# The last of three forward Fourier transforms goes from split half precision to float32 products with the data as stationary operand

## What is computed

```
def _L3_conv_ref(x, weights):
    x_f = jnp.fft.rfft2(x)
    k_f = jnp.fft.rfft2(weights)
    out_f = jnp.einsum('bchw,ochw->bohw', x_f, k_f)
    return jnp.fft.irfft2(out_f, s=(H, W))
...
x = x + _L3_conv_ref(_gn(x), L3_conv_weights)
```

## Time and profile before

| | |
|---|---|
| median of 3 runs | 950.18 us (949.63 to 953.7) |
| the profiled execution | 949.47 us, span 947.6 us |
| busy over the span | TensorE 82%, VectorE 63%, ScalarE 55%, GpSimd 13% |
| mean granted clock of TensorE | 0.937 of full speed |

### The profile page before, as it was taken

How to read it: one execution, slowest core, us unless ns; L and a number is a source line. 1 busy time by engine, 2 the same in 40 slices (tenths; PEclk the granted TensorE clock), 3 DMA queues, 4 the chain that set the end, 5 groups by cost and what they waited for, 6 DMA issues and landing times. The chain is left out here.

```text
span 947.6 us, 27147 instructions
## 1 busy us (share of the span) xinstructions
PE 780.6 (82%) x10775; PEld 652.6 (69%) x10775; DVE 599.3 (63%) x1112; ACT 518.9 (55%) x868; POOL 122.4 (13%) x120
## 2 busy tenths in 40 slices
PE   7999996875699464888599999966888488889998
PEld 7999995764588332766444444435777488879997
DVE  3455436678476697689687776775666677752222
ACT  0233337754534270755579998005887557755654
POOL 0000000110100162455103223000000100001110
PEclk9999998898799797889799999997999789999999
DMA  8599968750000100000000000004000448831222
GB/s 308 225 317 382 308 195 215 168 116 4 2 0 0 41 1 0 2 0 0 1 1 1 1 1 1 1 1 107 1 0 0 89 91 183 188 72 54 103 106 93
DMA packets 46066, 80.08 MB, mean 85 GB/s; under 512 B 19619, under 2 KB 38057, under 8 KB 41145
## 3 DMA queue, kind: packets, MB, share of 16 engines
q1 hardware_dynamic: 29368, 62.49, 23.5%
q10 hardware_dynamic: 16640, 16.78, 5.2%
HBM read 50.74 MB, written 27.92 MB: 83 GB/s over the span
## 5 line engine op out<-in xcount | busy, mean ns | idle before, releaser
L1478 DVE SCALAR_TENSOR_TENSOR X<-bank,c_power,X 32x512 f32 x128 | 96.7, 755 | 36.5 <-PE bank L1428 32.9
L930 DVE TENSOR_TENSOR X<-X,bank 128x512 f32 x64 | 43.7, 683 | 91.8 <-PE bank L916 91.8
L1621 PE MATMUL bank<-m_xp,m_kf 128*32 128x64 f32 x2048 | 79.2, 241 | 21.4 <-DVE m_xp L1556 10.0
L1621 PEld LDWEIGHTS bank<-m_xp,m_kf 128*32 128x32 f32 x2048 | 78.2, 171 | 22.7 <-issue 22.5
L433 ACT COPY ks_spec<-bank 128x512 f32<-128x512 f32 x64 | 34.3, 591 | 95.3 <-PE bank L360 92.3
L215 DVE BATCH_NORM_STATS2 bn<-X 128x6 f32 x128 | 83.2, 684 | 2.9 <-POOL X L1218 1.6
L415 DVE COPY ks_rows<-bank 128x512 f32<-128x512 f32 x64 | 41.2, 687 | 66.0 <-PE bank L345 66.0
L1384 ACT ACTIVATE c_r<-X,c_nrm 32x1024 f32 (+1 forms) x56 | 75.4, 1346 | 2.4 <-DVE c_nrm L1452 1.1
L345 PE MATMUL bank<-ks_fw,ks_src 64*128 64x64 f32 x1024 | 68.7, 298 | 6.5 <-DMA ks_src<-in_L_conv_weights 6.5
L345 PEld LDWEIGHTS bank<-ks_fw,ks_src 64*128 64x128 f32 x1024 | 68.1, 215 | 6.4 <-issue 6.4
L360 PE MATMUL bank<-ks_fh,ks_rows 64*128 64x128 f32 (+1 forms) x1152 | 71.1, 277 | 0.4 <-ACT ks_spec L433 0.4
(11 more groups left out here) (189 smaller groups left out, 1870.5 us busy)
## 6 DMA issues: line engine op xcount, KB each, us to landing
ks_src<-in_L_conv_weights SPq DMA_DIRECT2D x16, 1024.0 KB, 7.0
kf<-ks_spec ACTq DMA_DIRECT2D x16, 1024.0 KB, 9.2
m_kf<-kf SPq DMA_DIRECT2D x32, 512.0 KB, 8.3
X<-in_x SPq DMA_DIRECT2D x4, 2048.0 KB, 12.9
out_y<-X SPq DMA_DIRECT2D x16, 512.0 KB, 2.7
l_wb<-in_L_conv_weights_r SPq DMA_DIRECT2D x4, 512.0 KB, 10.8
l_wb<-in_L_conv_weights_i SPq DMA_DIRECT2D x4, 512.0 KB, 13.2
xf<-f_xm SPq DMA_DIRECT2D x16, 112.0 KB, 3.4
```

The costliest lines, as they stand in the source:

```text
L930: dve.tensor_tensor(x, x, ps[4 + c % 4][:], ALU.add).then_inc(added, 1)
L1478: dve.scalar_tensor_tensor(x, of.rearrange("p (y x) -> p y x", x=HN), filt.power[at, 2:3], x, ALU.mult, ALU.add).then_inc(added, 1)
L1621: last = pe.matmul(ps[4 * half + m // 8][at:at + C, m % 8 * N:(m % 8 + 1) * N], kf[p][:, j, :, H * half + m], xp[half][:, j, m].rearrange( ...
```

## The change

The last forward transform no longer uses `Forward`. All of it is in float32:

- The row and column matrices are float32 and come as ks_fw (32 KB), l3_fh and l3_fh0 (256 KB each, the matrix repeated for each row quarter) instead of three pairs of halves (64 KB each).
- f3_src is a ring of four chunks instead of a whole group. Chunks go through only two PSUM banks (0 and 1). A single copy takes the turned chunk to f3_tt, in an order in which each channel's 4 images x 32 rows lie together. Even chunks are copied by ScalarE, odd ones by VectorE.
- Row products: for each channel two products, on partitions 0 to 63 and 64 to 127, with the data as stationary operand (64 x 128) and the matrix moving (64 columns). Eight channels at a time, into banks 2 and 3; VectorE copies bank 2, ScalarE bank 3. The result already has the channels where the column products need them, so there is no second transposition.
- Column products: for each set of 4 slots, 4 parts x 4 images, each on a quarter of 32 partitions, data stationary (32 x 128), matrix moving (128 columns), image b into bank 4 + b, four products added up. Slot 0 has 16 more with 32 stationary columns. Four sets fill the four banks; then VectorE copies banks 4 and 5, ScalarE banks 6 and 7 to xm, each bank with the same step of 128 bytes.
- TensorE's order: a group's eight turns; then its four row blocks of 8 channels, between which the column products of the group before lie (sets 0 and 1 after the first block, 2 and 3 after the second, 4 and 5 after the third); the next group's turns; sets 6 and 7 of the group before. The last group's eight sets come at the end.
- The loop over the groups is written out instead of a hardware loop.

```diff
+    for k in ("l3_fh", "l3_fh0"):
+        out[k] = np.tile(out[k].reshape(C, 2, 2, P), (IB, 1, 1, 1))
...
-        fwd = Forward(pr, ctx, "f3", mats, SLOT_AT, True, {2: 0, 4: 1, 6: 2, 8: 3}, {9: 4, 10: 5, 12: 6, 14: 7})
+    RING, GROUPS, SETS = 4, 4, 2
+    ready_by = [0, 1, 0, 1, 0, 1, 0, 0]
+    read_by = [1, 0, 1, 0, 1, 0, 1, 0]
...
+        src = pr.sb(ctx, "f3_src", [P, RING, CH])
+        tt = pr.sb(ctx, "f3_tt", [P, C, IB, N // 2])
+        rows = [pr.sb(ctx, f"f3_rows{p}", [P, 2, 2 * SLOT, C]) for p in range(2)]
...
+                def turn(q, j):
+                    n = NCH * q + j
+                    pe.wait_ge(ready[ready_by[j]], count(ready_by, ready_by[j], q, j))
+                    if n >= 2:
+                        e = read_by[(n - 2) % NCH]
+                        pe.wait_ge(turned_read[e], count(read_by, e, (n - 2) // NCH, (n - 2) % NCH))
+                    for k in range(4):
+                        m = pe.transpose(ps[n % 2][:, k * P:(k + 1) * P], src[:, n % RING, k * P:(k + 1) * P],
+                                         pr.ident[:])
+                    m.then_inc(turned, 1)
+                def transform_rows(q, g):
+                    n = GROUPS * q + g
+                    for e in range(2):
+                        if g == 0:
+                            pe.wait_ge(turned_read[e], read_by.count(e) * (q + 1))
+                        if n:
+                            pe.wait_ge(rows_read[e], n)
+                    for c in range(C // GROUPS):
+                        for half in range(2):
+                            at = slice(half * N, (half + 1) * N)
+                            m = pe.matmul(ps[2 + half][:, c * N:(c + 1) * N],
+                                          tt[at, C // GROUPS * g + c].rearrange("p b h -> p (b h)"), fw[at],
+                                          start=True, stop=True)
+                    m.then_inc(rows_made, 1)
+                def transform_columns(q, f):
+                    n = SETS * q + f // 4
+                    for e in range(2):
+                        if f == 0:
+                            pe.wait_ge(rows_read[e], GROUPS * (q + 1))
+                        if f % 4 == 0 and n:
+                            pe.wait_ge(kept[e], 2 * n)
+                    def products(slots, mat):
+                        for i, (half, part) in enumerate(np.ndindex(2, 2)):
+                            for b in range(IB):
+                                at, pos = slice(b * C, (b + 1) * C), SLOT * part + 4 * f
+                                m = pe.matmul(ps[4 + b][0:slots * C, f % 4 * P:(f % 4 + 1) * P],
+                                              rows[q % 2][at, half, pos:pos + slots].rearrange("p s c -> p (s c)"),
+                                              mat[at, half, part], start=i == 0, stop=i == 3)
+                        return m
+                    m = products(4, fh)
+                    if f == 0:
+                        m = products(1, fh0)
+                    if f % 4 == 3:
+                        m.then_inc(cols_made, 1)
+                pr.keep_warm(pe, 7)
+                for j in range(NCH):
+                    turn(0, j)
+                for q in range(Q):
+                    for g in range(GROUPS):
+                        transform_rows(q, g)
+                        if q and g < 3:
+                            transform_columns(q - 1, 2 * g)
+                            transform_columns(q - 1, 2 * g + 1)
+                    if q + 1 < Q:
+                        for j in range(NCH):
+                            turn(q + 1, j)
+                    if q:
+                        transform_columns(q - 1, 6)
+                        transform_columns(q - 1, 7)
+                for f in range(SLOT // 4):
+                    transform_columns(Q - 1, f)
...
+            def keep(eng, copy, e, q, u):
+                eng.wait_ge(cols_made, SETS * q + u + 1)
+                for b in (2 * e, 2 * e + 1):
+                    copy(xm[:, 4 * u:4 * u + 4, :, :, IB * q + b].rearrange("p f k r -> p f r k"),
+                         ps[4 + b][:].rearrange("p (f r k) -> p f r k", f=4, r=2)).then_inc(kept[e], 1)
+            def copies(eng, copy, e):
+                def turn(q):
+                    for j in range(NCH):
+                        copy_turned(eng, copy, e, q, j)
+                        if j + RING < NCH:
+                            normalise(eng, e, q, j + RING)
+                for j in range(RING):
+                    normalise(eng, e, 0, j)
+                turn(0)
+                for q in range(Q):
+                    for g in range(GROUPS):
+                        copy_rows(eng, copy, e, q, g)
+                        if g == 0 and q + 1 < Q:
+                            for j in range(RING):
+                                normalise(eng, e, q + 1, j)
+                        if g == 1 and q:
+                            keep(eng, copy, e, q - 1, 0)
+                    if q + 1 < Q:
+                        turn(q + 1)
+                    if q:
+                        keep(eng, copy, e, q - 1, 1)
+                for u in range(SETS):
+                    keep(eng, copy, e, Q - 1, u)
...
-                fwd, fwd_loads = matrices(pr, inner, [(n, [P, 2, P]) for n in ("l3_fw16", "l3_fh16", "l3_fh016")], F16)
+                fwd, fwd_loads = matrices(pr, inner, [("ks_fw", [P, N]), ("l3_fh", [P, 2, 2, P]), ("l3_fh0", [P, 2, 2, P])])
```

More of the change, by code:

```diff
@@ L1487, in l3_forward_stage, with count @@
 def l3_forward_stage(pr, mats, xm, kf0, loaded0):
+    nc, ps = pr.nc, pr.psum
+    fw, fh, fh0 = mats
+    RING, GROUPS, SETS = 4, 4, 2
+    turned, rows_made, cols_made = (pr.sem(f"f3_{n}") for n in ("turned", "rows_made", "cols_made"))
+    ready, turned_read, rows_read, kept = ([pr.sem(f"f3_{n}{e}") for e in range(2)] for n in (
+        "ready", "turned_read", "rows_read", "kept"))
+    ready_by = [0, 1, 0, 1, 0, 1, 0, 0]
+    read_by = [1, 0, 1, 0, 1, 0, 1, 0]
+    def count(by, e, q, j):
+        return by.count(e) * q + by[:j + 1].count(e)
     with ExitStack() as ctx:
-        fwd = Forward(pr, ctx, "f3", mats, SLOT_AT, True, {2: 0, 4: 1, 6: 2, 8: 3}, {9: 4, 10: 5, 12: 6, 14: 7})
-        with pr.nc.Block() as block:
+        src = pr.sb(ctx, "f3_src", [P, RING, CH])
+        tt = pr.sb(ctx, "f3_tt", [P, C, IB, N // 2])
+        rows = [pr.sb(ctx, f"f3_rows{p}", [P, 2, 2 * SLOT, C]) for p in range(2)]
+        with nc.Block() as block:
             @block.sync
@@ new lines, in _, with normalise @@
+                for f in range(SLOT // 4):
+                    transform_columns(Q - 1, f)
+            def normalise(eng, e, q, j):
+                if ready_by[j] != e:
+                    return
+                n = NCH * q + j
+                if n >= RING:
+                    eng.wait_ge(turned, n - RING + 1)
+                of, to = pr.X[:, q, j * CH:(j + 1) * CH], src[:, n % RING]
+                if e:
+                    done = eng.activation(to, of, ACT.Identity, scale=pr.rstd[:, q:q + 1], bias=pr.shift[:, q:q + 1])
+                else:
+                    done = eng.tensor_scalar(to, of, pr.rstd[:, q:q + 1], pr.shift[:, q:q + 1], ALU.mult, ALU.add)
+                done.then_inc(ready[e], 1)
@@ new lines, in copy_turned, with copy_rows @@
+            def copy_turned(eng, copy, e, q, j):
+                if read_by[j] != e:
+                    return
+                n = NCH * q + j
+                eng.wait_ge(turned, n + 1)
+                copy(tt[:, :, :, 4 * j:4 * j + 4],
+                     ps[n % 2][:].rearrange("p (h b c) -> p c b h", h=4, b=IB)).then_inc(turned_read[e], 1)
+            def copy_rows(eng, copy, e, q, g):
+                eng.wait_ge(rows_made, GROUPS * q + g + 1)
+                at = slice(C // GROUPS * g, C // GROUPS * (g + 1))
+                copy(rows[q % 2][:, e, :, at],
+                     ps[2 + e][:].rearrange("p (c n) -> p n c", n=2 * SLOT)).then_inc(rows_read[e], 1)
@@ L1501, in _ @@
             @block.vector
             def _(dve):
-                fwd.low_parts(dve)
+                copies(dve, dve.tensor_copy, 0)
             @block.scalar
             def _(act):
-                fwd.high_parts(act, lambda q, s: act.copy(
-                    xm[:, s, :, :, bass.ds(IB * q, IB)].rearrange("p k r b -> p b r k"),
-                    pr.psum[4 + s % 4][:].rearrange("p (b r k) -> p b r k", b=IB, r=2)))
+                copies(act, act.copy, 1)
 def load_kernel_spectra(sp, pr, to, i, pair, loaded):
```

7 lines of the change are left out of this document (2 added, 5 removed).

## The result

The changed kernel takes 969.55 us (median of 4 runs, 966.13 to 974.55) against 949.9 us (4 runs, 949.15 to 953.7): 1.0193 times as long, 95% interval 1.0159 to 1.0227. It is slower, as forecast, but by 19.6 us instead of 5.3, and outside the range of 945 to 966. The profiled execution took 968.98 us, 19.5 more than that of before.

A forecast was written before the change was run, and what follows sets the result against it. The last forward transform was taken as a chain through TensorE, ScalarE and VectorE, no engine full. Stage +3.35, matrices +0.6, early slow clock +0.4 and tail clock fall +1.7 gave +6.05: 955.5 us profiled from 949.47; range 945 to 966.

The forecast's parts named there:

- The row and column prices: Last forward transform: row products at 0.056 us a record, column products on four quarters at 0.028.
- rival B: Column products: quarters not four times as fast; no better than halves +32, 988 us; halfway +9, 965; chance 0.13.
- halfway: Column products at 0.036 us a record, quarters gaining only part of the speed: +9, 965 us.
- rival C: Last forward transform: shape changes between row tiles cost nothing, not 0.17 us each; -4.1, 951.4 us, no change; chance 0.22.
- rival D: More waiting: VectorE's scattered xm copy at 1.28 us (+4.4), or clock falls in turn stretches; 960 to 963; chance 0.13.
- (g): Larger forward matrices, 352 KB more, loaded in the stats stage ahead: +0.6 us, bounds 0 and 1.2.
- four R, with the row copies uncovered between them: Group 0: four row blocks of 1.79 us with three copy waits of 0.97 between them, 10.07 us.
- Item (i): Tail: TensorE idles 2.2 us twice, one clock fall of 3.2 us counted: +1.7 us, bounds 0 and 3.4.
- turn stretch: A group's eight turns through two banks: 5.11 us of TensorE's queue, 5.28 with a change of shape.
- Keep waits: Column sets share the same four banks, so the next set waits 2.23 us for copies to xm.
- (c): Copy prices: VectorE 0.69 us, ScalarE 0.59; scattered xm copy 1.10, two in 1.95; VectorE's bounds 0.69 and 1.28.
- The first stretch: From the stage's first transposition to its first row product: 6.48 us.

The follow-up runs named there:

- the second trace: The changed kernel run and traced once more, with nothing altered: 970.43 us, ratio 1.0190 to the kernel before.
- Runs 1 and 2: Changed kernel with, first, idle transpositions filling group 0's waits, 963.31 us; second, group 0's row products alternating banks 2, 3 and 4, 5, 958.94 us.
- run 7: Changed kernel plus alternating row banks in group 0, last group's first column sets in banks 0 to 3, two-image xm copies, four-bank turns: 947.21 us, ratio 0.9947.

## Why the prediction was wrong

**What held.** The direction, and the shape of the argument: scarce banks turn work that overlapped into waits. The row and column prices: 0.029 us a record against 0.028 (rival B is refuted by the steady rows; its "halfway" price, 0.036, was not halfway between 0.028 and 0.056, which is 0.042, and nothing hung on it). Changes of shape cost what was forecast, against rival C: in the steady group 702.91 - 700.91 = 2.00 us less 64 x 0.0286 leave 0.17 behind column products, and a row block, 1.93 from its start to the next products (685.13 to 687.06), less 32 x 0.056 leaves 0.14. The 3.07 times that the Trainium skill's table gives for four row tiles (TensorE: Matmul & The Clock Gate, Measured speedup vs the span model) did not show here: against the 0.113 of a product on 128 rows, 0.0286 is 4.0 times as fast, at 128 columns where the table has 512. Turns with gaps (before the third, the fifth and the eighth, where every second one was forecast), waits of 2.2 us twice in the tail, the clock low once behind them at 1.6 us (5.48 against 3.85): nearly as written. In the second trace the clock fell behind both waits, so "once" was in part luck. One of the two waits is put down to VectorE's xm copy, which was rival D's sign: it takes 1.16 us, just over the 1.10 up to which it was to hide. The matrices cost 0.8, within (g)'s bounds.

**The step that failed** is group 0's: "four R, with the row copies uncovered between them (4 x 1.79 + 3 x 0.97 = 10.07)". The waits were priced right and taken for plain idle time. Item (i) let the clock fall only behind idle times of 2 us, because the two examples in the trace of before were of that size. Waits of 0.78 and 0.79 us ahead of two blocks of 2.00 did it as well, and what followed ran at half speed for 13.7 us: two row blocks 1.68 longer each, and the turn stretch 7.73 instead of about 6.25, together 4.8 of the 5.1 us missed there. Runs 1 and 2 show it. The Trainium skill (TensorE: Matmul & The Clock Gate, A second HAM failure mode: psum-queue depth-cycling) describes a case of this kind, in another number format: short idles between groups of products that cycle through PSUM banks, and a clock that goes up and down. The trace agrees in that idle times of 0.79 us sufficed; here it fell once and stayed down. Rival D named the clock, but in the turn stretches, at 0.13; it should have looked at row blocks, and had a larger chance.

**Terms mis-sized.** Keep waits: 2.6 us each (0.17 and 2.43 from row block to column products) against 2.23. (c) took ScalarE's copy at 1.10 with two in 1.95, from a copy that only ScalarE did; in the changed kernel's tail, with both engines at it, a pair takes 2.15 to 2.19, on both. Whether the company is the reason was not tried. A steady turn stretch took 5.57 against 5.28. The first stretch, to the first row product, took 7.00 against 6.48. The first three make up the 0.6 to 1.1 us in each later group, and use up the 1.1 that a steady group was to gain.

**A premise.** "The mix stage starts only behind its end, so a microsecond of this stage is one of the kernel" holds for the start, not for the length of what follows. The mix stage grew by 2.4 us in the first pair of traces: 1.8 in its products (81.0 against 79.2) and 0.6 in waits. The forecast put it at nothing. Its instructions are the same. What in the new stage ahead of it makes its waits fall differently was not found. Behind the start of its products, where both kernels have the lower clock, the changed kernel has two more low stretches of about 3.4 us; one in the windows:

```profile
857.70:861.10 3.40, 3.40 (x65) 3.40 (x67) 1.45 (x4) 1.12 (x2) 0.00 (x0) 0.50 0.00 0
```

It stands behind a wait of 3.12 us for kernel spectra, of the uneven kind; the other, from 796.2, behind the pause of 2.00.

The change itself was not a bad idea: with four more edits, all of them of banks and of the order of a copy's elements, the same products make a kernel 0.5% faster than the one before.

## What to carry to other kernels

When a rewrite takes work off TensorE, count the banks before the products: a bank that is written, copied and written again puts a wait of one copy and two hand-overs on TensorE, and such waits close together may cost the clock too: here two of 0.79 us did, and the fall cost nearly 5 us. Where banks of a later phase stand free in an earlier one, lend them. And try whether a copy that scatters can write two adjacent floats; here it took 0.5 us off each.

## What the runs showed of the hardware, not expected

- The clock fell with two waits of 0.78 and 0.79 us and one block of 2.0 us just behind it, in all six traces that have them, and stayed low for 13.7 us in the first.
- It also fell, and mostly stayed down, with TensorE busy for 232 of 250 us, when products on one quarter of the rows followed each other (0.58 in the mean); with the same products on the four quarters by turns the page of the changed kernel shows it at 9 tenths or more (slices 29 and 30).
- Copies of 512 floats from PSUM that write 4 bytes every 128 take 1.16 us on VectorE and 1.19 on ScalarE, and 0.69 and 0.68 if they write 8. The forecast's bound for VectorE, 1.28, was near; its reasoning, that ScalarE's factor (1.10/0.59) holds on VectorE, gives too much: 1.16/0.69 is 1.7, not 1.9.
- Waits for loads of one total fell evenly (1.6 us each) or on every second pair (3.0), the same way in every trace of one program; what decides it was not found. The even kind never cost clock; of the long ones all three did in run 7, and one of three in the changed kernel.
